# A two-layer cross-attention kernel: layer-0 values folded with the layer-1 query weights by columns, earlier layer-0 scores of the second block, and other orders in the last block

## The reference

```python
# layer 0 (single head, masked, residual)
q = x @ Wq.T + bq ;  k = y @ Wk.T + bk ;  v = y @ Wv.T + bv
scores = where(mask == 0, NEG, q @ k.T)
x1 = softmax(scores) @ v + x
# layer 1 (16 heads of 32, output projection, residual, LayerNorm)
Q = x1 @ W1q.T + b1q ;  K = y @ W1k.T + b1k ;  V = y @ W1v.T + b1v
context = softmax(Q_h @ K_h.T / sqrt(32)) @ V_h
out = layernorm(context @ Wo.T + bo + x1) * gamma + beta
```

## Time and profile before

| | |
|---|---|
| median of 3 runs | 371.81 us (371.07, 371.81, 374.77) |
| profiled execution | 373.18 us, of which the span is 371.1 us |
| PE busy | 358.8 us, 97% of the span |
| DVE, ACT, POOL busy | 259.2, 253.4, 225.6 us |
| mean granted TensorE clock | 0.987 of full speed |
| chain that ended last | PE 86%, ACT 5%, DVE 3%, DMA 3% |

### The profile page before, as it was taken

One profiled execution on the slowest core, in us unless ns is written; L12 is line 12 of the kernel. 1 busy time (PEld: TensorE's weight loads), 2 busy tenths in 40 slices (PEclk: granted clock), 3 DMA queues, 4 the chain that ended last, 5 costly groups with the idle time before them and its releaser, 6 DMA issues.

```text
span 371.1 us, 17166 instructions
## 1 busy us (share of the span) xinstructions
PE 358.8 (97%) x7288; PEld 278.7 (75%) x7288; DVE 259.2 (70%) x591; ACT 253.4 (68%) x1190; POOL 225.6 (61%) x248
## 2 busy tenths in 40 slices
PE   8999999899999999999999999999999999999894
PEld 7969876667777777777777777777777777677673
DVE  0345567657777769776977687876877696757756
ACT  1343789858767876877687776897687768767500
POOL 0520356665543988388837886488838882896642
PEclk9999999999999999999999999999999999999978
DMA  8954732230131322304240324132232203052113
GB/s 290 385 200 133 256 89 84 90 112 4 61 119 35 113 91 66 117 31 143 65 148 4 115 88 141 44 115 89 81 100 68 79 3 105 31 198 61 58 58 114
DMA packets 19111, 38.82 MB, mean 105 GB/s; under 512 B 2238, under 2 KB 3774, under 8 KB 18907
## 3 DMA queue, kind: packets, MB, share of 16 engines
q1 hardware_dynamic: 18296, 36.72, 29.6%
q10 hardware_dynamic: 739, 1.01, 0.9%
HBM read 26.49 MB, written 8.39 MB: 94 GB/s over the span
## 4 chain that ended last, share of the span: by engine, by line
PE 86%; ACT 5%; DVE 3%; DMA 3%; issue 2%; SPq 1%; POOL 0%; DVEq 0%
PE ps_qo L1174 27%; PE ps_qo L1263 23%; PE ps_mid L1202 11%; PE ps_mid L1190 5%; ACT prob L621 4%; PE ps_qo L1126 4%; PE ps_hi L1190 2%; PE ps_mid L1281 2%; PE ps_mid L1089 2%; PE ps_qo L1324 2%; PE ps_hi L1281 1%; DMA v<-v 1%; PE ps_mid L1102 1%; PE ps_hi L1089 1%; DMA raw<-in_w0k 1%
## 5 line engine op out<-in xcount | busy, mean ns | idle before, releaser
L459 POOL TENSOR_TENSOR prob<-prob,rc 128x308 f32<-128x308 f32 x128 | 92.5, 724 | 98.9 <-DVE rc L866 96.7
L621 ACT ACTIVATE prob<-ps_mid,mx 128x77 f32<-128x77 f32 x256 | 79.3, 335 | 47.5 <-DVE mx L847 47.3
L621 ACT ACTIVATE prob<-ps_hi,mx 128x77 f32<-128x77 f32 x256 | 80.1, 379 | 0.0
L621 ACT ACTIVATION_READ_ACCUMULATOR prob<-ps_hi,mx 128x1 f32 x256 | 66.6, 260 | 0.0
L859 DVE STREAM_TRANSPOSE pt<-prob 128x768 f32<-128x768 f32 x64 | 61.9, 968 | 6.4 <-PE ps_mid L1202 4.9
L621 ACT ACTIVATION_READ_ACCUMULATOR prob<-ps_mid,mx 128x1 f32 x256 | 54.8, 214 | 0.0
L1174 PE MATMUL ps_qo<-x_h,wq_h 128*128 128x512 f32 x128 | 53.4, 417 | 0.0
L1174 PE MATMUL ps_qo<-x_h,wq_l 128*128 128x512 f32 x128 | 51.2, 400 | 0.0
L866 DVE RECIPROCAL rc<-sm 128x4 f32<-128x4 f32 x128 | 22.3, 175 | 39.7 <-ACT prob L621 39.1
L1202 PE MATMUL ps_mid<-pt,v 32*32 32x128 f32 (+1 forms) x2976 | 48.1, 278 | 1.8 <-issue 0.8
L434 POOL TENSOR_TENSOR x_l<-x_raw,x_h 128x512 fp32r<-128x512 f32 x32 | 41.0, 1305 | 14.6 <-ACT x_h L563 11.9
(11 more groups left out here) (133 smaller groups left out, 682.9 us busy)
## 6 DMA issues: line engine op xcount, KB each, us to landing
x_raw<-in_xT SPq DMA_DIRECT2D x14, 512.0 KB, 3.8
y<-in_x SPq DMA_DIRECT2D x28, 256.0 KB, 3.9
out<-y SPq DMA_DIRECT2D x28, 256.0 KB, 2.2
mask_sb<-in_mask SPq DMA_DIRECT2D x8, 154.0 KB, 3.8
raw<-in_w0q SPq DMA_DIRECT2D x4, 256.0 KB, 6.1
x_raw<-in_xT SPq DMA_DIRECT2D x1, 1024.0 KB, 8.4
raw<-in_w0v SPq DMA_DIRECT2D x1, 1024.0 KB, 10.3
raw<-in_w1q SPq DMA_DIRECT2D x1, 1024.0 KB, 13.3
```

The costliest lines, as they stand in the source:

```text
L459: nc.gpsimd.tensor_tensor(ap, ap, wide(rc[:, k % 2, h], KEYS), ALU.mult).then_inc(prob_done, 1)
L621: e = nc.scalar.activation(prob[:, k % 2, t, h, 0:KEYS], ps_s[h][:, t * KEYS:(t + 1) * KEYS], ACT.Exp, bias=mx[:, k % 2, h, t:t + 1], accu ...
```

## The change

1. **The fold by columns.** `fold` is gone. PE makes u transposed for both batches at once, `project(bank[3:5], raw2, v0T, mm_uT, ...)`: 16 matmuls of 154 columns. ACT copies it to SBUF in two pieces (`uT_leave`), PE turns it to rows with 8 transposes (`to_rows`), and ACT and DVE leave and split both batches in the prologue. One pair of transfers stacks both.
2. **Layer-0 scores of block 1** are made whole at the end of step 0. Their softmax stands earlier: `exp0(0, 1)` between the exponentials of heads 2 and 3 in step 1, `layer0_probs(0, 1)` at the end of DVE's step 1, `round_p0(0, 1)` one head earlier in step 2.
3. **The last block.** `normalise` of tiles 2 and 3 of block 5 moves from step 28 to step 29; in DVE's steps 28 to 30 `ct_rest` moves ahead of the transposes, and the second transpose of a unit follows its first instead of opening the next step. In the last step `last_residual(0)` moves ahead of the statistics, and `ct_rest(31)` ahead of `last_residual(1)`.
4. SP may load the first two row tiles of block 0 one step earlier, and doesn't wait for `u_stacked` of batch 1 any more.

```diff
@@ ACT, prologue
+            def uT_leave(n):
+                act.wait_ge(mm_uT, n + 1)
+                src = bank[3 + n][:, 0:2 * BATCH * KEYS].rearrange("p (e k) -> p e k", e=2)
+                nc.scalar.activation(uT[:, 2 * n:2 * n + 2], src, ACT.Copy).then_inc(uT_ready, 1)
...
+            uT_leave(0)
+            uT_leave(1)
+            round_p0(0, 0)
             round_u(0)
-            round_p0(0, 0)
+            round_u(1)
@@ ACT, first_step
                     exps(0, k, h)
-                    if k == 2 and h == 2:
+                    if k == 1 and h == 2:
+                        exp0(0, 1)
+                    if k == 2 and h == 1:
                         round_p0(0, 1)
-                if k == 2:
-                    round_u(1)
...
                 if k == 1:
-                    exp0(0, 1)
                     round_x(0, 1, 2, CH)
@@ ACT, step
-                if g == 0:
+                if g == 0 and b < LAST or g == 1 and b == LAST:
                     normalise(i, b - 2, 2)
                     normalise(i, b - 2, 3)
@@ DVE, first_step
                 if k == 1:
-                    inverse_sums(0, k, 1)
-                    inverse_sums(0, k, 2)
                     layer0_leave(0, 1)
                     layer0_mask(0, 1)
-                    inverse_sums(0, k, 3)
+                    inverse_sums(0, k, 1)
                     layer0_select(0, 1)
                     layer0_shift(0, 1)
+                    inverse_sums(0, k, 2)
+                    inverse_sums(0, k, 3)
+                    layer0_probs(0, 1)
@@ DVE, step
+                if b == LAST:
+                    ct_rest(i, k - 1)
                 if g == 0:
                     variance(i, b - 2, 1)
                 transposes(i, k, 0)
-                ct_rest(i, k - 1)
-                if k == UNITS - 2:
+                if b == LAST:
                     transposes(i, k, 1)
+                else:
+                    ct_rest(i, k - 1)
@@ DVE, last_step
                 transposes(0, k, 1)
+                last_residual(0)
                 statistics(0, LAST - 1, 3)
                 variance(0, LAST - 1, 1)
-                last_residual(0)
                 ct_rest(0, k - 1)
@@ PE, prologue and first_step
-            fold(0, 0, CH)
+            project(bank[3:5], raw2, v0T, mm_uT, [ld_w1q, ld_w1q])
...
             query(0, 0, 0, 4)
+            pe.wait_ge(uT_ready, 2)
+            for v in range(BATCH):
+                to_rows(rows_of_u[v], uT, v, mm_u)
...
+            pe.wait_ge(u_ready, BATCH)
             project(bank[1:3], raw0, ctxT_sb, mm_k1T, [ld_w1k, ld_w1k], 1, CH)
-            pe.wait_ge(u_stacked[0], 32)
-            pe.wait_ge(u_copied, 1)
+            pe.wait_ge(u_stacked, 32)
+            pe.wait_ge(u_copied, BATCH)
...
-                    layer0(0, 1, 0, 2)
+                    layer0(0, 1)
                 if k == 1:
                     query(0, k + 1, 0, QUERY)
-                    layer0(0, 1, 2, TILES)
                 if k == 2:
-                    pe.wait_ge(add0_done, 2)
-                    fold(1, 0, CH)
                     query(0, k + 1, 0, 4)
```

More of the change, by code:

```diff
@@ L156, in xattn_kernel @@
         u_copied, v0_copied = sem("u_copied"), sem("v0_copied")
-        u_stacked, v0_stacked, p0_stacked = [sem("u_stacked0"), sem("u_stacked1")], sem("v0_stacked"), sem("p0_stacked")
+        u_stacked, v0_stacked, p0_stacked = sem("u_stacked"), sem("v0_stacked"), sem("p0_stacked")
         v1_spread, pad_zero, half_done = sem("v1_spread"), sem("pad_zero"), sem("half_done")
@@ L161, in xattn_kernel @@
         mm_k0T, mm_a0, mm_c0, mm_v0T = sem("mm_k0T"), sem("mm_a0"), sem("mm_c0"), sem("mm_v0T")
+        mm_uT, uT_ready = sem("mm_uT"), sem("uT_ready")
         mm_v0, mm_u, mm_k1T, mm_v1T, mm_v1 = sem("mm_v0"), sem("mm_u"), sem("mm_k1T"), sem("mm_v1T"), sem("mm_v1")
@@ L346, in stack_probs @@
                 move(p0_b[KEYS:BROWS, b % 2], p0_a[TAIL:KEYS, b % 2], p0_stacked)
-            stack_weights(u_a, u_b, slice(0, 1), u_stacked[0], u_ready, 1)
+            stack_weights(u_a, u_b, slice(0, BATCH), u_stacked, u_ready, BATCH)
             sp.wait_ge(p0_stacked, 32)
@@ L372, in step @@
                     stack_probs(i, b + 1)
-                    stack_weights(u_a, u_b, slice(1, 2), u_stacked[1], u_ready, 2)
                 if k == CH:
@@ L378, in step @@
                 if g == 0:
-                    wait(sp, s_done, units(i, k) + (k == CH))
+                    wait(sp, s_done, units(i, k))
                     load_rows(i, b - 1, 0)
@@ L384, in step @@
                     store(i, b - 2, 1)
+                    if k == CH + 1:
+                        sp.wait_ge(s_done, k + 1)
                     load_rows(i, b - 1, 2)
@@ L808, in u_rest @@
                 dve.wait_ge(u_h_ready, b + 1)
-                if b == 1:
-                    dve.wait_ge(v0_stacked, 32)
-                nc.vector.tensor_tensor(rest[:, b], ps_out[0:KEYS, :], f32(u_a[0:KEYS, b]), ALU.subtract).then_inc(u_ready, 1)
+                nc.vector.tensor_tensor(rest[:, b], rows_of_u[b][0:KEYS, :], f32(u_a[0:KEYS, b]), ALU.subtract).then_inc(u_ready, 1)
             def u_again(b):
@@ L826, in _ @@
             wq_rest(1)
+            p0_rest(0, 0)
             u_rest(0)
-            p0_rest(0, 0)
+            u_rest(1)
             u_again(0)
+            u_again(1)
             dve.wait_ge(ld_bo, 16)
@@ L838, in _ @@
                 dve.wait_ge(v0_h_ready, v + 1)
-                dve.wait_ge(u_stacked[0], 32)
+                dve.wait_ge(u_stacked, 32)
                 nc.vector.tensor_tensor(rest[:, v], v0o[:, v], f32(v0_a[0:KEYS, v]), ALU.subtract).then_inc(v0_ready, 1)
@@ L946, in first_step @@
                 if k == 2:
-                    layer0_probs(0, 1)
+                    transposes(0, k - 1, 1)
                     inverse_sums(0, k, 1)
-                    transposes(0, k - 1, 1)
+                    p0_rest(0, 1)
                     inverse_sums(0, k, 2)
-                    p0_rest(0, 1)
                     inverse_sums(0, k, 3)
-                    u_rest(1)
-                    u_again(1)
                     transposes(0, k, 0)
@@ L974, in step @@
                     ct_rest(i, k - 2)
-                transposes(i, k - 1, 1)
+                if b < LAST or g == 0:
+                    transposes(i, k - 1, 1)
                 if g == 1:
@@ L1028, in last_step @@
                 transposes(0, k, 1)
+                last_residual(0)
                 statistics(0, LAST - 1, 3)
                 variance(0, LAST - 1, 1)
-                last_residual(0)
                 ct_rest(0, k - 1)
                 offset(0, LAST - 1, 1)
+                ct_rest(0, k)
                 last_residual(1)
-                ct_rest(0, k)
                 last_residual(2)
@@ L1154, in query @@
                     wait(pe, q_ready, units(i, k))
-                if k == CH and first <= 3 * CH < last:
-                    pe.wait_ge(u_stacked[1], 32)
-                    pe.wait_ge(u_copied, 2)
                 for m in range(first, last):
@@ L1319, in _ @@
             pe.wait_ge(c0_ready, 1)
-            def fold(b, first, last):
-                for c in range(first, last):
-                    mm = nc.tensor.matmul(ps_out[0:KEYS, :], v0T[:, c, b * KEYS:(b + 1) * KEYS], raw2[:, c],
-                                          start=(c == 0), stop=(c == CH - 1))
-                if last == CH:
-                    mm.then_inc(mm_u, 1)
             project(bank[1:3], raw0, ctxT_sb, mm_k1T, [ld_w1k, ld_w1k], 0, 1)
```

4 lines of the change are left out of this document (3 added, 1 removed).

## The result

The changed kernel takes 375.48 us (median of 20 runs, 372.04 to 377.38), the kernel before 372.58 us (20 runs measured with them, 370.06 to 374.77). The ratio is 1.0069, 95% interval [1.0041, 1.0098]: slower by 0.4 to 1.0%, within the 1% that the forecast counted as the same. A second measurement of the same two kernels, among the experiments, gave 1.0079 [1.0051, 1.0107]. The ratios leave out the few runs that lie over 1.5% above the fastest of their kernel, and they are not quotients of the medians, which here would give 1.0078 and, the second time, 1.0096. The forecast was 373.6 against 371.81, a ratio of 1.0048: the direction is right, and the size is 0.8 to 1.1 us short of the +2.6 and +2.9 us that the two ratios make of 372.6 and 372.8 us.

The account below looks back on a forecast made before the run. PE was taken to bound the kernel, unbroken from 73 to about 313 us, with ACT bounding steps 1 and 2. 2.65 - 0.9 = +1.75 us took the median from 371.81 to 373.6, between 371.4 and 376.0; with rivals, 368.6 to 376.0.

Parts of the forecast that it names:

- The fold by columns in the prologue, +1.64: Prologue on PE: projecting matmuls 4.20 and transposes 0.87 replace the first fold's 3.43, on the path, +1.64 us.
- The cover of the stacked u: Prologue: 12 projecting matmuls, 3.15 us, hide the stacking transfers; taken as zero, up to 0.5 us if it fails.
- Layer-0 half moved, +1.21: Second half of block 1's layer-0 scores moves from step 1 to step 0, delaying unit 1's scores by 1.21 us.
- Steps 1 and 2, -0.2: From unit 1's scores to unit 3's, 18.30 us bounded by ACT: saved copies nearly offset by a new wait, -0.2 us.
- The new wait before `exp0`: Step 1: ACT waits 0.6 us for DVE before the layer-0 exponential between heads 2 and 3.
- ACT alone as the bound: Steps 1 and 2: ACT, busy 11.93 of 12.00 us from 48 to 60 us, sets the pace.
- The last block, -0.9: Last block: 0.4 us gained around unit 29's scores and 0.5 us before the last output, together -0.9 us.
- The sum: Whole kernel: 2.65 us late at unit 3's scores less 0.9 in the last block, +1.75 us.
- the clock falls in step 2: Rival, chance 0.16: PE idles about 3 us in step 2, the clock falls, 2.2 us reach the path, 375.8.
- 5 to 28: Steps 5 to 27: taking another time than before would show the forecast wrong.
- the granted clock, the other sign named there: A granted clock differing between the two traces before 80 us or after 350 us would show the forecast wrong.
- The fall at the end: Rival, chance 0.13: the halved wait before the last output lets the clock hold, 3.2 us go, 370.4.

Follow-up runs that it names:

- e4_wo: Changed kernel with ACT's two roundings of the output weights in step 2 moved behind the rounding of unit 3's query; 376.62 us, ratio 1.0079 to the kernel before.
- e6_x: Changed kernel with ACT's four roundings of block 1's x moved from step 1 to step 0; 375.4 us, ratio 1.0063 to the kernel before.
- e1_last: Kernel before with only the last block's new orders on ACT and DVE; 370.31 us, ratio 0.9941 to the kernel before.
- e9_fill3: e1_last plus four matmuls with unused results in step 3 before unit 4's scores; 371.91 us, ratio 0.9952 to the kernel before.
- e10_dve: Changed kernel with block 1's x rounded in step 0 and DVE's layer-0 probabilities behind unit 2's maxima; 376.23 us, ratio 1.0085 to the kernel before.
- e8_fill2: Changed kernel with unused matmuls filling PE's waits: eight in step 2, two and four more in step 1; 375.13 us, ratio 1.0027 to the kernel before.
- e2_fold: Kernel before with only the fold by columns, layer-0 scores in halves and old softmax and last-block orders; 374.91 us, ratio 1.0066 to the kernel before.
- e7_best: Kernel before with the edits of e2_fold, e1_last, e4_wo and e6_x together, layer-0 scores in halves; 376.77 us, ratio 1.0089 to the kernel before.
- e5_fill: Changed kernel with eight matmuls with unused results in PE's 2.12 us wait of step 2; 377.64 us, ratio 1.0105 to the kernel before.
- before again: Second profile of the kernel before, unchanged, measured against itself; ratio 1.0004.
- e3_l0: Kernel before with only block 1's layer-0 scores whole in step 0 and the matching softmax orders, both folds by rows; 375.08 us, ratio 1.0068.

## Why the forecast was nearly right, point by point

- **The fold by columns in the prologue, +1.64.** The start of unit 0's scores also holds the slow first matmuls, so the stretch from the start of the fold to unit 0's scores is the measure: 12.31 or 12.32 us in all five profiles without the fold by columns, 14.14 to 14.43 in the nine with it, +2.0 between the means. Up to the first query matmul it is +0.76, as the sum had it (4.20 - 3.43); the rest is +1.1 to +1.35 us, where the sum had 0.87 for the transposes. They take 0.79 themselves. (The 2.2 us that the forecast sets beside its 0.87 multiplies the length of one transpose by eight. One does last 0.27 us in this trace, but they overlap and start 0.11 us apart.) The cover of the stacked u, which the forecast called thin, is used up: in the changed kernel the transfer ended at 38.30 and PE's matmuls at 38.29, and in e4_wo and e6_x PE waited 0.20 us for it.
- **Layer-0 half moved, +1.21.** +1.07, in every profile.
- **Steps 1 and 2, -0.2.** 18.35 and 17.98 us against 18.30, or against the 18.50 and 18.66 of e1_last and e9_fill3, which have the same code there: -0.7 to 0. The new wait before `exp0` was 0.44 us for the 0.6 forecast. The number held, the reason held in part. I had ACT alone as the bound, from its 11.93 busy us of 12. In the changed kernel, whose step 1 starts later, it is busy 7.93 of these 12 us (3.1 us of the rest is a wait for unit 1's maxima, whose scores start later), and e4_wo, e6_x and e10_dve show that what PE waits for is a ring: scores, DVE's maxima behind the layer-0 probabilities and a transpose, ACT's exponentials, the query. I never costed that the change also puts `layer0_probs`, 1.1 us of DVE, ahead of unit 2's maxima.
- **The last block, -0.9.** -1.05: 0.46 around unit 29 (0.4 forecast), 0.59 in the last step (0.5 forecast). Around unit 29 it went as argued: the wait for `ct_rest` is gone, from the start of unit 28's scores to that of unit 29's 0.6 us, and 0.2 of it came back as a longer wait for ACT's exponentials. In the last step the forecast had `ve` wait for something that ends at about 350.4 us; that is POOL's addition, see the last section. The best-founded part of the forecast.
- **The sum** of these four, measured, is 2.0 + 1.07 - 0.2 - 1.05 = +1.8 us, and was forecast as +1.75. That they agree so well is in part luck, since the fold costs 0.35 more and the last block gives 0.15 more than forecast. What is missing to the +2.6 and +2.9 lies in two terms that I had at zero. The range, too, was added up wrongly: from its own bounds it is 371.81 + 2.85 with 0 to 1.5, -0.8 to +0.1 and -1.6 to 0, which gives 372.3 to 376.3 us and not 371.4 to 376.0.
- **First missing term: the clock.** The rival "the clock falls in step 2" was a real part of the case, not an alternative to it. The granted clock over all comparable runs has the mean 0.993 in the kernel before (90 runs) and 0.985 in the changed one (32 runs). Of those 90 runs 21 had 0.998 or more, of these 32 none. In the kernel before the runs of 0.998 and more have a median of 370.7 us, those up to 0.987 of 375.0. In the changed kernel a fall costs less, if it comes in steps 1 or 2: PE waits there anyway, and 1 to 3 with a fall in it took 17.98 us. One in steps 3 and 4 reaches the path: 3 to 5 took 21.38 us in the second profile, with a clock of 0.77 and 0.66 in the stretches from 72 to 84 us. Of the 2.9 us above the first profile up to 1.94 are the standstill in which that fall began:

```profile
75.97 0.66 PE L1212 MATMUL ps_mid<-pt,v 13*32 13x128 f32 x11 [1.94 <-issue]
```

  I had given this rival +2.2 us at 0.16; some fall in these steps is in eight of the nine profiles with the fold by columns, and in three of the five without. Filling the holes raised the mean clock to 0.9945, and by the ratios it brought back 1.6 to 1.9 us (1.0027 in place of 1.0069 and 1.0079); its interval overlaps both of theirs, so the gain in time is likely and not shown. The three runs of e8_fill2 at 0.998 and more have a median of 372.5 us, 1.8 above those of the kernel before at that clock, which is the sum of the four terms. But the mean clock is not the whole of the rest: from 0.984 to 0.988 the 18 runs of the changed kernel range from 372.1 to 377.8 us. By the Trainium skill (TensorE: Matmul & The Clock Gate, "HAM oscillation — how this bites in real kernels") waits between bursts throttle the engine; the case it describes has waits for data that are longer than the work between them. Here they are far shorter than the work, and the clock fell all the same, in some executions and not in others.
- **Second missing term: 5 to 28.** I had said that another time there would prove me wrong, and it was another, as was the granted clock, the other sign named there: 228.5 to 229.5 us in the five profiles without the fold by columns, 228.7 to 231.6 in the nine with it, 1.5 us more in the mean. That alone is more than is missing, so these profiles don't settle how it is shared between the two terms. PE's instructions there are the same. The additional time lies in single units, 0.2 to 1.4 us each, some marked as "issue", in four profiles one of 0.3 to 0.6 us as a wait for the second stacking transfer of p0:

```profile
117.22 0.47 PE L1184 MATMUL ps_qo<-p_a,u_a 122*128 122x512 f32 x1 [1.16 <-issue]
```

  One kernel with the fold by columns (e6_x) has next to none of it, and the units differ between two profiles of the same kernel. Standstills without a releaser are not new with the change: the kernel before has one of 0.85 us at 79.45 us, where the forecast read its chain as unbroken. One piece can be tied to the code. SP issues the two stacking transfers of p0 one right behind the other, but in all nine profiles with the fold by columns, and in none of the five others, the second one for block 4 (at about 190 us) comes 0.4 us late, and PE waits 0.3 to 0.6 us for it in three of them (changed, e2_fold, e7_best). On SP's queue before, and now:

```profile
186.37 0.87 SPq L332 DMA_DIRECT2D p_a<-p_a  x1
187.28 0.56 SPq L332 DMA_DIRECT2D p_b<-p_a  x1
```

```profile
192.35 0.85 SPq L335 DMA_DIRECT2D p_a<-p_a  x1
193.66 0.56 SPq L335 DMA_DIRECT2D p_b<-p_a  x1
```

  What holds SP up there, and what makes up the rest, stays open.
- **The fall at the end** went away in the first profile and was back in the second. As far as fourteen profiles tell, it isn't tied to the wait that the change shortens, so the rival was no rival but a share of the executions of either kernel.

## What to carry to other kernels

When work leaves an engine's queue, list what it was covering on each other engine; the fold hid DVE's whole layer-0 softmax, and busy shares name the fullest engine, not the ring of waits that sets the pace. Price a stretch from at least two profiles of the same kernel where the clock or the first matmuls may differ, and start it at the first instruction that the change touches: differences between starts that repeat to 0.1 us are the code, the others are the execution. And an edit bundled with others is worth trying alone: here one part gave 1 us, and each of the other two cost at least as much.

## What the runs showed of the hardware

- The clock can fall around waits that are short and lie within a busy stretch: 1.88 us (e5_fill), 2.12 us (changed kernel, first profile). The same wait often brings no fall. Ten profiles have a wait of 1.01 to 1.06 us before unit 4's scores. In six the clock fell within about 1.3 us of its end (before again, e1_last, e2_fold, e6_x, e10_dve, e7_best), in four it stayed at 1.00 (before, e3_l0, e5_fill, e8_fill2).
- A small DVE operation (128 x 2 elements) takes 0.77 us or 0.18 in the same role, by when it runs: right behind the aggregation in both orders, but with `last_residual` ahead of the three it starts 0.92 us and not 2.11 us before the last output. What it waited for can be read beside it: POOL's addition of 128 x 512 elements. On POOL before, and now:

```profile
349.17 1.26 POOL L481 TENSOR_TENSOR y<-y,rows_sb 128x512 f32<-128x512 f32 x1
```

```profile
355.70 1.27 POOL L485 TENSOR_TENSOR y<-y,rows_sb 128x512 f32<-128x512 f32 x1
```

  In all four profiles with the old order `ve` starts about 0.7 us before the end of this addition and itself ends 0.02 to 0.04 us after it (350.46 after 350.43). In the ten with the new order it starts only 0.15 us before that end and takes 0.17 to 0.19 us. That `ve` waits for the addition is read from these times; no run moved the addition alone.
- The start isn't fixed either: the first projecting matmuls took 1.23 us for four instead of 0.69 until about 9 us in three of fourteen profiles (changed, e5_fill, e8_fill2), and unit 0's scores start at 39.97 to 40.05 us there, against 37.7 to 38.9 in the six others with the same prologue. It looks like a lower clock, but the granted clock of those profiles reads 1.00 from 0 to 12 us, so the record does not show the cause.
